# Moving 27 of 43 weight chunks behind the seam of a two-stage fp8 feed-forward kernel, with another way to turn the activations

## What is computed

```python
xm = x * cmask                                  # channels of the batch's session
h  = gelu(einsum('bct,bch->bht', xm, W_sess[ids]) + b_sess[ids])   # 256 hidden rows
o  = (einsum('bht,hs->bst', h, W2) + b2) * tmask                   # 128 x 2048 a batch
w_q = (weight * 448 / amax(weight)).astype(float8_e4m3fn)          # 2048 x 2048
x_q = (o * 57344 / amax(o)).astype(float8_e5m2)
out = x + (x_q @ w_q.T) / x_scale / w_scale + bias
```

## Time and profile before

| | |
|---|---|
| median of 3 runs | 839.88 us (838.34 to 839.89) |
| the profiled execution | 837.83 us, of which the span is 836.0 us |
| granted TensorE clock, mean | 0.998 |
| TensorE busy | 821.8 us, 98% of the span |
| VectorE, ScalarE, GpSimd busy | 482.6, 339.9, 514.8 us |
| chain that ended last | TensorE 93% (second-stage matmuls alone 51%) |
| DMA | 222 MB, mean 266 GB/s |

### The profile page before, as it was taken

One profiled execution on the slowest core, in us unless ns is written; L12 is line 12 of the kernel. 1 busy time (PEld: TensorE's weight loads), 2 busy tenths in 40 slices (PEclk: granted clock), 3 DMA queues, 4 the chain that ended last, 5 costly groups with the idle time before them and its releaser, 6 DMA issues.

```text
span 836.0 us, 10119 instructions
## 1 busy us (share of the span) xinstructions
PE 821.8 (98%) x3523; PEld 481.1 (58%) x3570; DVE 482.6 (58%) x503; ACT 339.9 (41%) x354; POOL 514.8 (62%) x233
## 2 busy tenths in 40 slices
PE   8899999999999999999999999999999999999998
PEld 5678888777677676765444444444444444444444
DVE  6989999888888888888552323232323323232322
ACT  7889999998898889883200000000000000000000
POOL 1998999889999999995983242424242424242322
PEclk9999999999999999999999999999999999999999
DMA  7799999878767877666974777676767686868682
GB/s 277 285 375 326 334 323 345 323 278 320 304 256 299 308 296 274 252 208 227 359 242 125 244 245 251 238 261 229 267 222 274 215 281 214 282 214 280 215 252 107
DMA packets 74864, 222.08 MB, mean 266 GB/s; under 512 B 37578, under 2 KB 39634, under 8 KB 55506
## 3 DMA queue, kind: packets, MB, share of 16 engines
q1 hardware_dynamic: 73936, 220.62, 74.9%
q10 hardware_dynamic: 898, 1.09, 0.4%
HBM read 144.35 MB, written 69.21 MB: 255 GB/s over the span
## 4 chain that ended last, share of the span: by engine, by line
PE 93%; DMA 2%; DVE 1%; ACT 1%; issue 1%; POOL 1%; SPq 0%; DVEq 0%
PE ps_h L1042 51%; PE ps_h L951 20%; PE ps_o L966 10%; PE ps_o L982 8%; PE ps_o L978 4%; DMA more<-more 1%; DMA x_sb<-in_x 0%; DMA wt<-in_L_cond_W_sess 0%; PE ps_h L1018 0%; POOL xl L514 0%; DVE hl L729 0%; ACT h L606 0%; ACT hh L597 0%; DVE whl L698 0%; ACT wqT L667 0%
## 5 line engine op out<-in xcount | busy, mean ns | idle before, releaser
L1042 PE MATMUL ps_h<-wqT,x_sb 128*128 128x512 bf16 x1877 | 411.3, 379 | 2.4 <-ACT x_sb L676 0.2
L1042 PEld LDWEIGHTS ps_h<-wqT,x_sb 128*128 128x128 fp8e5 x1920 | 187.4, 98 | 224.7 <-ACT x_sb L676 0.3
L514 POOL TENSOR_TENSOR xl<-x_sb,xh 128x1024 fp32r<-128x1024 f32 x62 | 149.5, 2411 | 14.4 <-ACT xh L591 14.4
L951 PE MATMUL ps_h<-xh,whl 128*128 128x512 f32 x508 | 150.4, 417 | 1.9 <-POOL whl L534 1.1
L557 POOL TENSOR_TENSOR x_sb<-x_sb,bias_sb 128x2048 f32<-128x2048 f32 (+1 forms) x15 | 66.7, 4446 | 133.1 <-DMA x_sb<-in_x 133.1
L557 POOL TENSOR_TENSOR h<-h,bias_sb 128x2048 f32<-128x2048 f32 (+1 forms) x15 | 66.6, 4442 | 123.2 <-DMA h<-in_x 123.2
L857 DVE SCALAR_TENSOR_TENSOR o_and_max<-ps_h,scales,h 128x512 f32<-128x512 f32 (+1 forms) x59 | 44.0, 746 | 137.4 <-PE ps_h L1042 137.4
L857 DVE SCALAR_TENSOR_TENSOR o_and_max<-ps_h,scales,x_sb 128x512 f32<-128x512 f32 x59 | 44.2, 750 | 134.6 <-PE ps_h L1042 134.6
L951 PEld LDWEIGHTS ps_h<-xh,whl 128*128 128x128 f32 x508 | 95.1, 188 | 39.8 <-issue 17.5
L739 DVE SCALAR_TENSOR_TENSOR o_and_max<-ps_o,b_sb,steps 128x1024 f32<-128x1024 f32 (+1 forms) x65 | 82.2, 1264 | 28.5 <-PE ps_o L982 26.9
L729 DVE TENSOR_TENSOR hl<-ps_h,hh 128x1024 fp32r<-128x1024 f32 x63 | 76.8, 1219 | 11.9 <-ACT ps_h L598 11.9
(11 more groups left out here) (100 smaller groups left out, 660.2 us busy)
## 6 DMA issues: line engine op xcount, KB each, us to landing
x_sb<-in_x SPq DMA_DIRECT2D x45, 1024.0 KB, 6.9
masked_out<-o_and_max SPq DMA_DIRECT2D x32, 1024.0 KB, 6.7
o_in<-masked_out SPq DMA_DIRECT2D x32, 1024.0 KB, 9.0
out<-o_and_max SPq DMA_DIRECT2D x27, 1024.0 KB, 5.1
wqT<-in_L_ffn_weight SPq DMA_DIRECT2D x23, 684.0 KB, 9.5
wt<-in_L_ffn_weight SPq DMA_DIRECT2D x40, 384.0 KB, 5.5
h<-in_x SPq DMA_DIRECT2D x14, 1024.0 KB, 7.2
wraw<-split_w SPq DMA_DIRECT2D x28, 256.0 KB, 6.9
```

Of the source, the lines that this page charges most:

```text
L514: pool.tensor_tensor(xl[:, u % 2, :], x_cols(u), xh[:, u % 2, :].bitcast(fp32), ALU.subtract)\
L951: mm = nc.tensor.matmul(to[:, cols], whl[:, b % DIRECT, rows], xs[:, u % 2, cols], start=(k == 0), stop=(k == 2))
L1042: mm = nc.tensor.matmul(bank, q[:, k // 2, :, k % 2], wq[:, n, k, cols], start=(k == 0), stop=(k == KT - 1))
```

## The change

The constants below set it. Scans take 768 columns, so there are 43 of them, one per unit, and `QUANT` becomes 45: 64 - 3 - 45 = 16 chunks are quantized before the seam and 27 behind it. `SPLIT_H1` is units 4 to 45.

```diff
-    DIRECT = 4
+    DIRECT = 6
+    RING = 4
+    SESS_AT = {0: (0,), 1: (1,), 2: (2, 3)}
+    STORE_AT = (4, 5)
+    RAW_AT = {3: 4, 5: 5}
+    SPLIT_LATE = {1: 2, 3: 3, 5: 4, 7: 5}
-    SPLIT_H1 = [u for u in range(1, 27)]
-    POOL_MASKS = 14
-    SCAN_COLS = 1368
+    SPLIT_H1 = [u for u in range(4, 46)]
+    POOL_MASKS = 24
+    SCAN_COLS = 768
-    CUT_TILES = (2, 2, 4, 4, 4)
+    CUTS = KQ
+    CUT = [slice(k * GROUP, (k + 1) * GROUP) for k in range(CUTS)]
-    QUAD = 4
-    FIRST = [(b, n) for b in range(QUAD) for n in range(NC - 1)] + [(b, NC - 1) for b in range(QUAD)]
+    QUAD, LEAD = 16, 6
+    EARLY_BANKS = 2
+    FIRST = [(b, n) for n in range(EARLY_BANKS) for b in range(LEAD)] \
+        + [(b, n) for b in range(LEAD, QUAD) for n in range(EARLY_BANKS)] \
+        + [(b, n) for n in range(EARLY_BANKS, NC) for b in range(QUAD)]
+    PIECES = len(FIRST) // 2
+    OWN, RINGP = 2, 6
+    AHEAD = 5
+    LATE_BEFORE = [0, 0, 2, 6, 6] + [p + 2 for p in range(5, 22)] + [25] + [27] * 9
+    CHUNK_BEHIND = [1, 2, 3, 4, 6, 8] + [2 * i - 6 for i in range(8, 20)] + [33, 35, 36, 38, 39, 41, 42]
+    QUANT_BEHIND = {2: 4, 3: 5, 5: 6, 7: 7, 8: 8, 9: 9, 10: 10, 11: 11, 12: 12, 13: 13, 14: 14, 15: 15}
+    MORE_O = (2, 3, 4, 5)
```

*The start.* Batch 1 of x is loaded in halves. The session weights are copied in four parts instead of one (`SESS_AT`), and loaded ahead of the raw weights of batches 2 and 3. Raw weights serve six batches; those of batches 2 to 5 are split by ScalarE and GpSimd in units 1, 3, 5 and 7 instead of by VectorE:

```diff
+            def low_session_weight(b):
+                pool.wait_ge(raw_masked, b - 1)
+                pool.tensor_tensor(whl[:, b % RING, HID:2 * HID], raw_sb[b], whl[:, b % RING, 0:HID].bitcast(fp32),
+                                   ALU.subtract).then_inc(wl_late, 1)
+            def high_session_weight(b):
+                act.wait_ge(raw_loaded[b], 16)
+                if b >= RING:
+                    act.wait_ge(h1_psum, (b - RING + 1) * UPB)
+                act.activation(whl[:, b % RING, 0:HID], raw_sb[b], ACT.Copy, scale=cmask[:, b:b + 1])
+                act.activation(raw_sb[b], raw_sb[b], ACT.Copy, scale=cmask[:, b:b + 1]).then_inc(raw_masked, 1)
```

*Loads of o.* Each is four DMAs that place 32 by 128-word squares, in pieces of 512 bytes, so that a 32 by 32 transpose of four-byte words finishes the turn. Six are loaded before the seam (issued at units 48, 50, 51, 53, 55 and 57), four of them into the half of the weight buffer that is not yet written:

```diff
-            def load_o(b, r):
-                sp.dma_start(o_in[:, r, :], masked_out[ds(b, 1), :, :].rearrange("a s t -> (a s) t"))\
+            def load_o(b, r, to=o_in, loaded=o_in_loaded):
+                squares = masked_out[ds(b, 1), :, :].rearrange("a (i c) (k g w) -> (a g) c k i w", c=SQUARE, k=KQ, g=4)
+                for g in range(4):
+                    sp.dma_start(to[g * SQUARE:(g + 1) * SQUARE, r, :].rearrange("c (k i w) -> c k i w", k=KQ, i=4),
+                                 squares[g]).then_inc(loaded[r], 16)
```

```diff
+            def quantize(b, loads, src=o_in, loaded=o_in_loaded, r=None):
+                ...
+                act.activation(q8[:, r % 2, :], src[:, r, :], ACT.Copy, scale=o_scale, saturate=False)\
+                   .then_inc(q_later_ready, 1)
+            def turn(r, to, count, words=slice(0, T // QUADS), ready=q_later_ready):
+                dve.wait_ge(ready, count)
+                dve.transpose(to[:, words], q_words[:, r, words]).then_inc(q_turned, 1)
             for k in range(CUTS):
                 quantize(0, 1, k == 0, CUT[k])
+                turn(0, qT_words[0], k + 1, slice(k * P, (k + 1) * P), q_ready)
+                if k == 1:
+                    round_at(EARLY_CHUNKS)
-                    mm = nc.tensor.matmul(bank, q[:, k // 2, :, k % 2], wq[:, n, k, cols],
+                    mm = nc.tensor.matmul(bank, q[:, k // QUADS, :, k % QUADS], wq[:, n, k, cols],
-            together = [n for b, n in FIRST[0:NC - 1]]
+            together = [0]
```

```diff
+            for p in range(PIECES):
+                for i in late[0 if p == 0 else LATE_BEFORE[p - 1]:LATE_BEFORE[p]]:
+                    round_chunk(i)
+                ...
+                if one_batch(p):
+                    pool.tensor_tensor(at, at, bias_sb[:, 0:UNIT], ALU.add).then_inc(xb_ready, 1)
+                else:
+                    for cols in HALVES:
+                        add = pool.tensor_tensor(at[:, cols], at[:, cols], bias_sb[:, n * BANK:(n + 1) * BANK], ALU.add)
+                    add.then_inc(xb_ready, 1)
```

More of the change, by code:

```diff
@@ new lines, in _ @@
+            load_piece(AHEAD - 1)
+            for p in range(PIECES):
+                store_piece(p)
+                if p + AHEAD < PIECES:
+                    load_piece(p + AHEAD)
+                if LEAD <= p + 4 < QUAD:
+                    sp.wait_ge(q_later_ready, p + 4)
+                    sp.wait_ge(o_stored[p % 2], ((p + 6) // 2 + 1) * 16)
+                    load_o(p + 6, p % 2)
+                if p in (QUAD, QUAD + 1):
+                    if p == QUAD:
+                        for k in range(OWN):
+                            sp.wait_ge(piece_stored[k], 16)
+                    load_x_again(p, p % 2)
@@ L467, in step2 @@
                     if not last:
-                        sp.wait_ge(q_ready, b + CUTS)
+                        sp.wait_ge(q_later_ready, b)
                         load_o(b + 2, r)
-                    if not (last and r == 1):
-                        sp.wait_ge(y_psum, b * NC + ONE)
-                        sp.sem_inc(load_turn, 1)
-                        sp.wait_ge(q_ready, b + 1 + CUTS)
-                        sp.sem_inc(transpose_turn, 1)
-                        turn(1 - r)
                     if last and r == 1:
@@ L496, in _ @@
             for r in range(2):
[L497 removed]
+                sp.wait_ge(y_stored[r], 16 * (STEPS - QUAD // 2 - r) + DMA)
             for n in range(NC + 1):
                 sp.wait_ge(y_chunk_stored[n], 16)
[L500 removed]
+            for k in range(OWN):
+                sp.wait_ge(piece_stored[k], 16)
+            for k in range(RINGP):
+                sp.wait_ge(piece_stored[OWN + k], (PIECES - OWN - k + RINGP - 1) // RINGP * 16)
         @block.gpsimd
@@ L686, in _ @@
                        .then_inc(wt_loaded[i % 3], 16)
+                if i - EARLY_CHUNKS in QUANT_BEHIND:
+                    b = QUANT_BEHIND[i - EARLY_CHUNKS]
+                    if b in MORE_O:
+                        quantize(b, 1, o_more, o_more_loaded, MORE_O.index(b))
+                    else:
+                        quantize(b, b // 2 + 1 - len(MORE_O) // 2)
+            quantize(QUAD, QUAD // 2 + 1 - len(MORE_O) // 2)
+            with act.Fori(QUAD // 2, STEPS - 1) as i:
+                for r in range(2):
+                    quantize(i * 2 + r + 1, i + r + 1 - len(MORE_O) // 2, r=1 - r)
+            quantize(B - 1, STEPS - len(MORE_O) // 2)
         @block.vector
@@ L845, in _ @@
-            quantize(1, 1, True, slice(0, T))
+            turn(1, qT_words[1], 1)
             dve.reciprocal(o_inv, o_scale).then_inc(scale_step, 1)
             dve.wait_ge(scale_step, 6)
-            dve.tensor_tensor(y_scale, o_inv, w_inv, ALU.mult).then_inc(scale_step, 1)
-            for i in late[1:4]:
-                exponents(i)
-                round_at(i)
+            dve.tensor_scalar(y_scale, o_inv, w_inv, None, ALU.mult).then_inc(scale_step, 1)
+            exponents(late[1])
+            round_at(late[1])
```

331 lines of the change are left out of this document (146 added, 185 removed).

## The result

| | before | after |
|---|---|---|
| median | 839.88 us (838.34 to 840.05, 4 runs) | **847.82 us** (846.73 to 848.48, 4 runs) |
| ratio after to before | | 1.0097 [1.008, 1.0115] |
| profiled execution, span | 837.8, 836.0 us | 847.3, 845.5 us |
| mean granted clock | 0.998 | 0.994 |

Slower by 7.9 us, where 12.3 less was forecast: 20.2 us from the predicted time, outside the range, with the other sign.

A forecast was written before the change was run, and what follows sets the result against it. TensorE was taken as the bound: matmul pace 810.2 us, the other 26 us start, seam and tail. Gains of 6.4 (split units), 4.7 (start) and 1.2 (seam), together 12.3, took the median 839.88 to 827.6 us; range 822 to 836.5.

The forecast's parts named there:

- part 3: Seam between the stages: quicker first product, fewer identity matmuls, no transpose wait, 2.4 us less 1.2 new cost, net 1.2.
- The loads rival: End of first stage: six o loads crowd x loads, 3 to 8 us reach TensorE, typically 832.6 us; chance 0.15.
- The sum was made for GpSimd: Second stage: 27 late chunks (91 us) and x+bias pieces (90) total 181 us, within TensorE's 221 for 64 groups.
- Split units: First stage, units 27 to 45: each split saves 0.337 us on TensorE, 6.4 us in all.
- Start: First units: halved batch 1, session copy in four, moved scalings and no early remainders save 6.2 us, net 4.7.
- The deduction: First units: weights' low parts in GpSimd's queue delay the next remainders, between 0 and 3 us, taken as 1.5.
- Seam: Between the stages: first product about 0.75 us after quantizing starts; gains of 2.4 us less 1.2, net 1.2.
- the deduction of 1.2: Between the stages: VectorE and GpSimd slow each other, the last cut waiting out a GpSimd step; 0 to 2 us.
- Strided reads: Second-stage products: rival that reading stationary fp8 at every fourth byte costs 32 us, giving 859.6 us; chance 0.09.
- ScalarE's quantizing: Second stage: 2048 columns take 1.93 us on ScalarE, beside 13.8 us of products per batch.
- GpSimd's chain: Behind the seam: rival that late GpSimd chunk steps hold TensorE, costing 3 to 5 us, 831.6 us; chance 0.11.

The follow-up runs named there:

- run 1: Changed kernel with each o loaded in one DMA of 128 rows of 8 KB, placing in squares left out: 828.79 us.
- run 3: Changed kernel with each o loaded in four DMAs over all 128 partitions in 512-byte pieces, squares left out: 828.39 us.
- run 6: Changed kernel with each o in four DMAs of 32 partitions, 512-byte pieces scattered in DRAM, squares left out: 850.07 us.
- run 7: Changed kernel with each o in four DMAs over 128 partitions, 512-byte pieces scattered in DRAM, squares left out: 827.41 us.
- Run 4: Changed kernel with the loads of o for batches 2 to 5 issued at units 24, 30, 36, 42 instead of 51, 53, 55, 57: 841.18 us.
- Run 9: As run 3, but units 27 to 45 no longer split: 833.18 us.
- run 11: Changed kernel with early o loads spread over units 24 to 42; from batch 8, SyncE loads partitions 0 to 63, ScalarE's queue 64 to 127: 826.99 us.
- run 8: As run 3, but GpSimd is handed its first late chunk after the fourth cut instead of the second: 827.76 us.
- run 15: The same kernel as run 11, measured again beside run 14 and another variant: 827.84 us.
- run 5: Changed kernel with the four DMAs of each o issued in the order 0, 2, 1, 3 instead of rising: 845.97 us.
- run 14: As run 11, but GpSimd is handed its first late chunk after the fourth cut instead of the second: 830.75 us.
- run 12: Changed kernel with the squares made when o is stored, by four 32-partition stores, and o loaded over 128 partitions per DMA: 828.92 us.
- run 2: Changed kernel with each o in four DMAs of 32 partitions but whole 8 KB rows, squares left out: 835.23 us.

## Why the prediction was wrong

**The step that failed** is the end of part 3, that four issues of 512-byte pieces cost "about 0.4 us of SP each, beside the products" and that "None of this moves the end". It charged the loads for their issues and put what they do to the transfers at nothing. By run 1 the form of the loads moved the end by 19.0 us. The price of an issue was wrong as well, but that was not the loss: in run 3 the four issues take 3.7 us (7.2 in the first stage), and TensorE has no wait for a turned batch there and 0.6 for `hl`. I did ask about the loads in a rival, but only of the length of the pieces, which costs no time while the DMAs are wide (run 3 against run 1), and not of the number of partitions that each DMA reaches (22.7 us, run 6 against run 7). Once the DMAs are narrow, the pieces count too: 835.23 with long rows, 847.82 with short ones. No row of before has a DMA of 32 partitions, so this was an operation that the trace does not show, and by the prediction's own method it should have had a bound on both sides.

**The loads rival** had the right place and size for the first stage: x landings over 11 us, TensorE waiting between 300 and 360, 3 to 8 us. It measured 7.9: of the gain of 9.9 at unit 46 (272.56 against 282.5) 2.0 are left at the seam, made of some 5.9 us of the `hl` waits and a granted clock of 0.91 over 20 us, 1.8. Run 4 takes it away. Its cause was wrong, and with it the agreement of its size is in part luck: it doubled the price of every byte for the pieces, where pieces alone took 0.13 of share on top of 0.60 and no time. Pieces of 512 bytes ran as fast as rows when the DMA was wide, 828.39 against 828.79 us. The Trainium skill ("DMA: Bandwidth & Descriptors", Specifications) has 512 B as the least size for full rate, by which the rival was empty as it stood. The times agree with it; the shares in the loop, 0.73 against 0.60 at 230 and 226 GB/s, don't quite.

**What no rival had** is the second place, behind the seam, 11.7 us: waits of 8.4, and 3.3 for the two batches at a lower granted clock (by the windows 1.8 for 0.91 from 480 to 500, 1.5 for 0.97 over the next 50). The sum was made for GpSimd over the whole of the 64 groups (181 of 221 us), but transfers were never summed per stretch. Batches 6 to 15 take a new batch of o every 6.9 us, twice the rate of the loop behind them, 13.8, and this stretch has x, outputs and chunks besides: 361 GB/s. Near the 385 of the earlier trace rows that holds only with loads that reach full rate.

By the profiled executions the miss is 21.8 us (847.3 against 825.5 forecast). The two places are 7.9 + 11.7 = 19.6 of it, the start 1.1; 1.1 us I can't place. The terms, one by one:

- *Split units*, 6.4 predicted: pace 5.553 as said. The gain grew from 3.6 us at unit 9 (66.03 against 69.64) to 9.9 at unit 46, so 6.3. Run 9 puts it at 5.5 to 6.0.
- *Start*, net 4.7 predicted: 3.6. Unit 3's hidden matmuls came at 22.37 (about 22.3 said), unit 7's output stood at 4.5 of gain, and the low parts of the weights took 0.9 of it by unit 9: the chain between units 4 and 9 goes through GpSimd, at 6.03 us a unit. The deduction was 1.1 too small. The start also varies: the gain at unit 9 is 1.9 us in the profiled execution of run 3 and 3.2 in that of run 11.
- *Seam*, net 1.2 predicted: in runs 3 and 11 the last product ends 445.8 us behind the broadcast, 1.1 sooner than before. The timeline of after's seam shows the steps:

```profile
385.51 0.49 DVE L907 TENSOR_SCALAR x_sb<-o_in,scales 128x512 fp8e5<-128x512 f32 x1 [0.17 <-DVE scales L900]
386.03 0.31 DVE L913 STREAM_TRANSPOSE x_sb<-x_sb 128x128 f32<-128x128 f32 x1
...
388.15 1.51 DVE L907 TENSOR_SCALAR x_sb<-o_in,scales 128x512 fp8e5<-128x512 f32 x1
...
392.26 0.70 DVE L913 STREAM_TRANSPOSE more<-x_sb 128x512 f32<-128x512 f32 x1
```

  The turn of a cut took 0.31 where I took 0.2, so the first product came 0.89 behind the quantizing's start (0.75 said). The last cut, beside GpSimd's step from 387.57, took 1.51 in place of 0.49, which is most of the deduction of 1.2 made visible. The turn of 512 words, 0.70, lies inside its bounds (0.48 to 0.96). By the Trainium skill ("GPSIMD Engine Reference", section 1) GpSimd and VectorE share SBUF interfaces when VectorE is in a two-port mode or has two SBUF inputs. That row agrees, though no view shows the mode.
- *Strided reads* (slower, 859.6): dead. The weight loads at stride four take what they took at stride two, and the products 0.2158:

```profile
L1105 PEld LDWEIGHTS ps_h<-wqT,x_sb 128*128 128x128 fp8e5 x1152 | 112.4, 98 | 137.1 <-DVE x_sb L913 3.3 <-POOL wqT L564 0.5
...
L735 ACT ACTIVATE x_sb<-o_in,scales 128x2048 fp8e5<-128x2048 f32 x27 | 53.9, 2001 | 293.4 <-DMA o_in<-masked_out 286.8
```

- *ScalarE's quantizing*, 1.93 predicted: 2.00. Its row shows what it waited for, 286.8 us for loads of o; most of that is idle time with nothing due, and the part that counts is in TensorE's waits.
- *GpSimd's chain*: no wait in after. Its margin was as thin as said: in run 8 the first late step of GpSimd begins 4.86 us behind the broadcast matmul in place of 3.44, and of these 1.4 us TensorE waits out 1.0 at the second bank.

With the loads repaired (runs 11 and 15) the rest of the change takes 826.99 to 827.84 us, on chips where the kernel before took 838.6 and 839.9. Their ratios, on the 839.88 of the forecast, give 828.0 to 828.5. So the forecast of 827.6 was right within a microsecond for the change without its narrow DMAs in one queue, and wrong for the kernel as written. As sums of the terms the gain there is 10.0 at the broadcast (11.1 predicted) and 1.1 behind it (1.2 predicted).

Open: why run 5's order and run 14's later chunk differ from what was expected, and why a second queue helps even in the same half. In time, pieces and width act together: narrow loads take 835.2 us with long rows and 847.8 to 850.1 with short pieces, wide ones 828 with either. In the share of the loop they nearly add. Why a narrow DMA holds the engines longer is not measured here.

## What to carry to other kernels

A DMA's price is also the set of partitions it reaches: split a load by columns (each DMA over all 128 partitions), not by groups of partitions. Where groups of 32 are forced, run two queues in opposite halves, rearrange when storing if that stage has the time (run 12), or spread the loads to where the engines have time. In a profile, a DMA share at its ceiling beside fewer GB/s than another stretch reaches at the same share is the sign. To price a form of load, compare the shares of two kernels where both move the same GB/s. When an order of work is changed, sum bytes per stretch against the time that the stretch has; an average over the stage hides that one part of it wants twice the rate.

## What was unexpected of the hardware

- That a narrow DMA holds the engines instead of leaving them free: with it the share is higher (1.13 against 1.05) while less is moved, and 0.94 against 0.73 where the same is moved. A busy share alone reads as work.
- An issue of a DMA in short pieces holds SyncE's queue: in after four issues of o took 3.9 to 8.2 us in the first stage and 5.1 to 6.0 in the second, and whatever stands behind them starts that much later. It goes with the pieces more than with the width: the four issues from 440 to 470 took 3.7 to 3.9 us in run 3 (wide, short pieces) and 1.8 to 1.9 in run 2 (narrow, long rows). By itself it cost nothing in run 3. From after:

```profile
315.19 8.02 SPq L389 DMA_DIRECT2D wqT<-masked_out  x4
```

And from run 3:

```profile
313.08 7.15 SPq L389 DMA_DIRECT2D wqT<-masked_out  x4
```

- Behind the two longest waits of TensorE, 3.02 and 2.86 us, the granted clock was lower: 0.73 from 480 to 485, and from 504 to 506 it was at the lower of its two levels, 1.2 of 2.4 GHz:

```profile
504.00:506.00 2.00, 2.00 (x6) 0.72 (x5) 0.59 (x1) 0.94 (x1) 2.00 (x2) 0.50 1.03 313
```

  The two batches took 8.71 and 8.75 us, where those behind the waits of 1.56 and 0.98 us took 7.07. That is 3.3 us on top of 8.4 us of waits.
